# Four graph networks on one core: empty edge places that index spread rows instead of row 0, and attribute scatters dealt out anew

## The chip, the cores and the metric

The kernel runs on one core of one Trainium2 chip, as one program. The metric is the time of one execution on the device in microseconds (us). Engines: PE (matmuls), DVE (VectorE), ACT (ScalarE), POOL (GpSimd, which here issues all indirect DMAs) and SP (SyncE, which issues all plain DMAs).

## The reference

Inputs are 6,250 nodes with 64 features `x`, 100,000 directed edges `src -> dst` (sorted by `dst`) and 18 attributes for each edge. Four networks follow each other; each adds its result to `x`, after a layer norm and a ReLU of its own input.

- Network 0: three layers; a node takes the mean of `h[src]` over its edges by `dst`, then two 64x64 matrices, a batch norm and an ELU.
- Network 1: two attention heads with a scalar score for each edge; sums by `src` of exp(score) times `h[dst]`.
- Network 2: a transformer with 128 hidden features, 8 heads and 4 layers; each layer has an attention over the edges (softmax by `dst`, keys and values gathered by `src`) and then a dense part (gate, layer norm, a 128-512-128 MLP with GELU).
- Network 3: attention with 4 heads, softmax by `src`, keys and values gathered by `dst`; the 18 attributes are projected and added to query, key and value of each edge.

## The kernel before

**Grouping.** Nodes are numbered in 49 blocks of 128 (NP = 6,272 places, 22 of them no node). Edges are padded to EP x ET = 128 x 784 = 100,352; the 352 filler edges have `src = dst = NP - 1`. The kernel sorts edges twice, by block of `dst` (table `tab[0]`, lists `idx[0]`, `node[0]`, `loc[0]`) and by block of `src` (`idx[1]`, ...). Each block's edges fill whole tiles of 128 edges, one edge to a partition, and T = 832 tiles are always processed. Counted from the inputs, 809 tiles hold edges in the order by `dst` (23 at the end are empty) and 810 in that by `src`; the last tile of most blocks is partly empty too, some 3,200 places in all. `idx[k]` holds the row of the node table that the place of an edge gathers. An empty place has local number -1, so that it matches no node, and its `idx` is 0: in order 0 because `fill0`, which `tab[0]` is filled with before edges are scattered into it, is zero in column 0; in order 1 because sums over no edge give 0 (`unpack_dve`, L1025).

**Passes.** A pass over the edges issues 832 indirect gathers from POOL, each 128 rows (one to a partition) into one of 4 buffers: `gathers` (L808) for the three layers of network 0 and for network 1, L1658 in `attend` for the four passes of network 2, L2643 for network 3. The rows are 384, 264, 1,024 and 384 bytes. SP waits for the gathers in the order of the tiles (`landed4` L815, `land_unit` L1676) and then raises a semaphore on which DVE or PE waits. In network 2 the same SP program also issues, behind these waits, the loads of the edge places (L837) and of the flags of the next step (L1666 to L1671), on which DVE's scan L1875 waits. In network 0 PE multiplies a one-hot of each tile by its gathered rows (L1137) and DVE adds (L1113); the third layer begins with `unpack_dve` on DVE. Between two passes lies a dense part, which is a block of its own: a block ends when all engines have ended.

**Attribute scatters.** Network 3 wants the pair and the attributes of each edge in order 1, in `tab[1]`. They are brought there in 49 chunks of 16 indirect scatters from POOL (L728), 784 in all, that are not needed before network 3. `SHARES` deals chunks to places where POOL has nothing else to do: 2 chunks in the dense part of network 0's last layer, 7 behind network 1's pass and in the block `n2i` after it, and 10 with each of network 2's four layers. Of a share of network 2, 32 scatters go behind the pass's gathers, and the rest in the dense block `after(l)`; their rows are loaded by SP (`load_early`: the row numbers and two chunks; `load_late`: the other chunks, two DMAs to a chunk, L701 and L702), and POOL waits for the whole late load before its first scatter in `after(l)`. SP ends `after(l)` with `cols.done`, a wait for all scatters (such waits, whose sums a helper keeps, show as L39).

**Network 1's norm.** The block before network 1's pass has no work for POOL. SP loads weights (L1388, L1389), stores two lists of node numbers (`store`, L1293), reads them back (`load`), and DVE, after the norm, compares them (L1330), builds two score terms with long `tensor_tensor` and `tensor_reduce` operations over 3,136 elements (L1425, L1426), and SP stores the node table (L1398).

Of the kernel before, what the change touches and what calls it, by code (L numbers as in the profile page):

```python
# [6 lines left out]
F32 = mybir.dt.float32  # L7
# [51 lines left out]
def build(nc, d):  # L59
    with ExitStack() as ctx:  # L60
# [40 lines left out]
        def io(pool, out, pat, cm):  # L101
            return pool.iota(out, pat, base=0, channel_multiplier=cm, allow_small_or_imprecise_dtypes=True)
# [45 lines left out]
        def group_edges():  # L148
# [59 lines left out]
            with ExitStack() as st, nc.Block() as block:  # L208
                sig = signals(nc, st, "keys")
                ld, v = sig("ld", 16), sig("v")  # L210

                @block.sync
                def _(sp):
                    for k in range(2):
                        sp.dma_start(ki[:, k, :], keys[k]).then_inc(ld.sem, 16)

                @block.gpsimd
                def _(pool):
                    io(pool, tio, [[1, T]], 0)

                @block.tensor
                def _(pe):
                    pe.matmul(R, zer[:, 0:HR], zer[:, :], start=True, stop=False, skip_group_check=True)

                @block.vector
                def _(dve):
                    v.on(dve.memset(fill, 0))
                    dve.memset(slot_t[:, ET:T], -1.0)
                    dve.memset(slot_p[:, ET:T], -1.0)
                    dve.memset(hi[:, :, ET:ET + 16], 0.0)  # L230
                    dve.memset(lo[:, :, ET:ET + 16], 0.0)
                    v.on(dve.memset(fill0, 0))
                    dve.wait_ge(v.sem, v.c)
                    dve.memset(fill[:, :, 0], -1)
                    dve.memset(fill0[:, :, 1], -1)
                    dve.tensor_scalar(triu, iota[:, :], pcol[:, 0:1], None, ALU.is_gt)
                    dve.wait_ge(ld.sem, ld.up(2))
                    v.on(dve.tensor_scalar(t1, ki, 6, None, ALU.arith_shift_right))
                    v.on(dve.tensor_scalar(ki, ki, LC - 1, None, ALU.bitwise_and))
                    dve.wait_ge(v.sem, v.c)  # L240
                    dve.tensor_copy(hi[:, :, 0:ET], t1)
                    dve.tensor_copy(lo[:, :, 0:ET], ki)
                    ld.back(dve)
                    v.back(dve)

                @block.scalar
                def _(act):
                    act.activation(junk[:, 0, 0:1], pcol[:, 0:1], ACT.Square)
# [484 lines left out]
                if self.n:  # L733
                    sp.wait_ge(sc[0].sem, sc[0].up(16 * self.n))

        SHARES = [0, 0, 2, 7, 10, 10, 10, 10]

        def share(i):
            return Share(sum(SHARES[0:i]), SHARES[i])
# [125 lines left out]
        def network0():  # L865
# [159 lines left out]
            def unpack_dve(dve, s):  # L1025

                def SS(ins):
                    s.on(ins)
                    dve.wait_ge(s.sem, s.c)

                o = STO
                blk, o = area(o, [128, T])
                num, o = area(o, [128, T], I32)
                low, o = area(o, [128, T], I32)
                t = low.bitcast(F32)
                pl = loc[1][:, 0:T]
                SS(dve.tensor_scalar(blk, pl, 128.0, None, ALU.mult))
                for q in range(2):
                    SS(dve.tensor_copy(num[:, 416 * q:416 * q + 416], SORTED[2 + q]))
                SS(dve.tensor_scalar(low, num, 3, None, ALU.bitwise_and))  # L1040
                SS(dve.tensor_copy(node[1][:, :], low))
                SS(dve.tensor_scalar(low, num, 2, None, ALU.arith_shift_right))
                SS(dve.tensor_copy(pl, low))
                SS(dve.tensor_scalar(pl, pl, -1.0, None, ALU.add))
                for q in range(2):
                    r = slice(416 * q, 416 * q + 416)
                    SS(dve.scalar_tensor_tensor(t[:, r], node[1][:, r], 2048.0, SORTED[q], ALU.mult, ALU.add))
                SS(dve.tensor_copy(idx[1][:, 0:T], t))
                SS(dve.scalar_tensor_tensor(blk, pl, 0.0, blk, ALU.is_ge, ALU.mult))
                SS(dve.tensor_tensor(node[1][:, :], blk, pl, ALU.add))  # L1050
                dve.memset(idx[1][:, T:T + 8], 0)
                SS(dve.memset(loc[1][:, T:T + 32], -1.0))
# [294 lines left out]
        def network1(ahead):  # L1347
            o = 0
            TB, o = area(o, [128, B, 66])
            X, o = area(o, [128, 4, 8, 66])  # L1350
            P, o = area(o, [128, 4, 8, 128])
            PT, o = area(o, [128, 2, 8, 128], BF)
            LB0, o = area(o, [128, 1024], BF)
            LB1, o = area(o, [128, 1024], BF)
            LB = [LB0, LB1]
            S3, o = area(o, [128, B, 6], BF)
            tmp, o = area(o, [128, B, 64])
            st_, o = area(o, [128, 4, B])
# [12 lines left out]
            with ExitStack() as st, nc.Block(no_gpsimd_drain=True) as block:  # L1371
                sig = signals(nc, st, "n1")
                v, vard, rootd, ld = sig("v"), sig("vard"), sig("rootd"), sig("ld", 16)
                built, stored = sig("built"), sig("stored", 16)

                f2 = Flags("n2f", sig, 0, 16, rows2, end, 0)
                f3 = Flags("n3f", sig, 1, 16, rows3, f2.o, 4)
                assert f3.o <= WORDS, f3.o

                @block.tensor  # L1380
                def _(pe):
                    f3.turn(pe)
                    f2.turn(pe)

                @block.sync
                def _(sp):
                    for q in range(2):
                        sp.dma_start(wv[:, q, :], bc(d["L1_gnn_W"][q][None, :], [128, 64])).then_inc(ld.sem, 16)  # L1388
                        sp.dma_start(wa[:, q, :, :].rearrange("p a f -> p (a f)"),  # L1389
                                     bc(d["L1_gnn_a"][q][None, :], [128, 128])).then_inc(ld.sem, 16)  # L1390
                    f3.store(sp)
                    f2.store(sp)
                    f3.load(sp)
                    f2.load(sp)
                    f3.finish(sp)
                    f2.finish(sp)
                    sp.wait_ge(built.sem, built.up())
                    sp.dma_start(table.rearrange("(b p) f -> p b f", p=128), TB).then_inc(stored.sem, 16)  # L1398
                    sp.wait_ge(stored.sem, stored.up())
                    built.back(sp)  # L1400
                    stored.back(sp)

                @block.scalar
                def _(act):
                    f3.copy(act)
                    f2.copy(act)
                    norm_act(act, vard, rootd, st_)
                    vard.back(act)

                @block.vector  # L1410
                def _(dve):
                    def VV(ins):
                        v.on(ins)
                        dve.wait_ge(v.sem, v.c)

                    f3.clear(dve)
                    f2.clear(dve)
                    norm_dve(dve, v, vard, rootd, h, x[:, :, :], 64, st_, tmp)
                    f3.compare(dve, v)
                    f2.compare(dve, v)  # L1420
                    dve.wait_ge(ld.sem, ld.up(4))
                    for q in range(2):
                        for s_ in range(2):
                            VV(dve.tensor_tensor(wa[:, q, s_, :], wa[:, q, s_, :], wv[:, q, :], ALU.mult))
                            VV(dve.tensor_tensor(tmp, h, bc(wa[:, q, s_, :][:, None, :], [128, B, 64]), ALU.mult))  # L1425
                            VV(dve.tensor_reduce(S1[:, :, q] if s_ == 0 else TB[:, :, 64 + q], tmp, AX.X, ALU.add))  # L1426
                    dve.sem_inc(built.sem, 1)

                    VV(dve.tensor_copy(S3[:, :, 0:2], S1))
                    VV(dve.tensor_tensor(S1, S1, S3[:, :, 0:2], ALU.subtract))  # L1430
                    VV(dve.tensor_copy(S3[:, :, 2:4], S1))
                    dve.tensor_tensor(S3[:, :, 4:6], S1, S3[:, :, 2:4], ALU.subtract)
                    for s in (v, rootd, ld):
                        s.back(dve)
# [146 lines left out]

            return acc, acc1

        first2 = share(3)
        sums1 = network1(first2)


# [394 lines left out]
        def network2(acc1, acc1b, cols0):  # L1982
# [535 lines left out]

            behind = [Share(sum(SHARES[0:4 + l]), SHARES[4 + l]) for l in range(4)]

            def preload_sp(l, sp, ld):
                sp.dma_start(Wp, d["W2all"][l][:, 512:1536]).then_inc(ld.sem, 16)
# [595 lines left out]
def prepare(inputs):  # L3120
# [2 lines left out]
    a = {}  # L3123

    fill = EP * ET - E
    src, dst = (np.concatenate([f(name), np.full(fill, NP - 1, f(name).dtype)]) for name in ("src", "dst"))
    a["src"], a["dst"] = src.reshape(EP, ET), dst.reshape(EP, ET)
    a["pair"] = np.stack([a["src"], a["dst"]], axis=-1)
    a["attr"] = np.concatenate([f("edge_attr_18"), np.zeros((fill, 18), np.float32)]).reshape(EP, ET, 18)
# [36 lines left out]
```

## Time and profile before

| | us |
|---|---|
| median of 3 runs | 12631.28 (12626.98 to 12631.36) |
| the profiled execution: its own time | 12619.18 |
| the profiled execution: span | 12617.4 |
| POOL busy | 8891.0 (70%) |
| DVE busy | 7916.2 (63%) |
| PE busy | 7549.2 (60%) |
| ACT busy | 6282.0 (50%) |

No engine is busy throughout, and the chain of waits that the page follows back from the end is short, so it does not tell what bounds the kernel. The profile is read stage by stage: which instruction of a stage ends last, and what it waited for. Gathers and scatters from POOL have the operation DMA_INDIRECT. A pause named "issue" is the engine's own time between two instructions.

### The profile page before, as it was taken

How to read it: one execution, taken by the hardware profiler on the slowest of the kernel's cores; microseconds unless marked ns; L12 is line 12 of the kernel's file. 1: busy time of each engine (PE TensorE's matmuls, PEld its weight loads, DVE VectorE, ACT ScalarE, POOL GpSimd, SP SyncE). 2: the span in 40 equal slices, each digit the busy share in tenths (PEclk: the TensorE clock that was granted, in tenths of full speed). 3: DMA queues.
4: the chain of work that ended last, by engine and by line, in shares of the span. 5: the costliest groups of instructions: out<-in, count | busy, mean ns of one | idle time of the engine just before them, and what ended most of it. 6: DMA issues, size and time to landing. Idle time of an engine off the chain costs nothing. (4 is left out here: it accounts for less than half of the span.)

```text
span 12617.4 us, 185971 instructions
## 1 busy us (share of the span) xinstructions
PE 7549.2 (60%) x46394; PEld 5746.9 (46%) x46395; DVE 7916.2 (63%) x21707; ACT 6282.0 (50%) x14083; POOL 8891.0 (70%) x9142
## 2 busy tenths in 40 slices
PE   6666455555551112343666676667666766667998
PEld 5666322232220002333466546663666366645766
DVE  8888666666662224333677767776777677775555
ACT  8333233333333333665566546664666366635666
POOL 0777677767767775777777677776777677766775
PEclk9766677767765555565777787778777877775555
DMA  0000111121121113223444544454444444432223
GB/s 33 2 2 2 31 39 39 39 38 39 39 38 39 40 40 48 54 53 52 132 132 132 118 111 133 131 125 105 132 133 132 96 133 131 133 74 58 72 71 63
DMA packets 820582, 949.30 MB, mean 75 GB/s; under 512 B 481147, under 2 KB 557360, under 8 KB 820156
## 3 DMA queue, kind: packets, MB, share of 16 engines
q0 software_dynamic: 343040, 637.31, 22.0%
q1 hardware_dynamic: 477244, 309.04, 9.2%
q14 instruction: 236, 1.93, 0.0%
q8 instruction: 62, 1.02, 0.0%
HBM read 859.26 MB, written 86.39 MB: 75 GB/s over the span
## 5 line engine op out<-in xcount | busy, mean ns | idle before, releaser
L808 POOL DMA_INDIRECT work<-t,idx x3328 | 3176.7, 955 | 1107.3 <-issue 1014.2
L1658 POOL DMA_INDIRECT work<-t,idx x3328 | 3177.6, 955 | 1024.0 <-issue 1013.4
L820 ACT ACTIVATE work<-iota,loc 128x128 f32<-128x128 f32 (+1 forms) x6672 | 2034.6, 387 | 3253.0 <-DVEq L1110 1921.9
L1113 DVE TENSOR_TENSOR work<-work,ps 128x192 f32 x2496 | 882.8, 354 | 1233.2 <-PE ps L1137 933.6
L1137 PE MATMUL ps<-work 128*128 128x192 bf16 x2496 | 412.7, 305 | 1764.1 <-SPq L815 1702.5
L1753 PE MATMUL ps<-work 128*128 x6784 | 1334.1, 379 | 140.9 <-ACT work L833 81.9
L1753 PEld LDWEIGHTS ps<-work 128*128 128x128 f32 x6784 | 1315.6, 297 | 179.5 <-issue 165.4
L1765 PE MATMUL ps<-work 128*128 128x136 f32 x6656 | 1264.8, 348 | 10.9 <-DVE work L1819 10.1
L600 POOL DMA_INDIRECT tab<-work x784 | 863.1, 1101 | 562.0 <-DVE work L453 315.0
L1137 PEld LDWEIGHTS ps<-work 128*128 128x128 bf16 x2496 | 232.4, 113 | 2077.8 <-issue 1069.8
L728 POOL DMA_INDIRECT tab<-work x784 | 818.7, 1044 | 462.7 <-issue 248.2
L1765 PEld LDWEIGHTS ps<-work 128*128 128x128 f32 x6656 | 1124.2, 246 | 23.2 <-DVE work L1819 15.2
L1849 DVE TENSOR_TENSOR work<-work,ps 128x512 f32<-128x512 f32 x848 | 580.2, 684 | 797.4 <-PE ps L1753 609.5
L2643 POOL DMA_INDIRECT work<-t,idx x832 | 804.7, 967 | 343.7 <-issue 250.2
L1021 PE MATMUL ps<-work 128*128 128x416 f16 x3328 | 995.4, 465 | 83.2 <-DVE work L1012 81.4
L1828 DVE TENSOR_TENSOR work<-work,ps 128x136 f32 x3328 | 939.1, 282 | 75.1 <-DVE work L1828 72.9
L824 ACT ACTIVATE work<-work,ones 128x1024 f32<-128x1024 f32 (+1 forms) x834 | 957.5, 1148 | 27.1
L1519 PE MATMUL ps<-work 128*128 128x130 f32 x1664 | 390.3, 428 | 624.0 <-DVEq L1563 624.0
L1819 DVE TENSOR_TENSOR work<-work,ps 128x512 f32<-128x512 f32 x832 | 567.3, 682 | 135.8 <-DVEq L39 82.5
L1519 PEld LDWEIGHTS ps<-work 128*128 128x128 f32 x1664 | 364.2, 331 | 630.1 <-issue 630.1
L833 ACT ACTIVATE work<-work,ones 128x1024 f32<-128x1024 f32 (+1 forms) x530 | 608.6, 1148 | 65.0 <-ACT work L830 3.4
L1021 PEld LDWEIGHTS ps<-work 128*128 128x128 f16 x3328 | 394.4, 125 | 509.1 <-issue 290.3
(426 smaller groups left out, 17006.6 us busy)
## 6 DMA issues: line engine op xcount, KB each, us to landing
work<-t,idx POOLq DMA_INDIRECT x7488
node<-pl SPq DMA_DIRECT2D x424, 256.0 KB, 3.4
work<-pl SPq DMA_DIRECT2D x54, 512.0 KB
work<-pl SPq DMA_DIRECT2D x106, 256.0 KB, 3.3
tab<-work POOLq DMA_INDIRECT x1568, 2.1
t<-work SPq DMA_DIRECT2D x196, 128.0 KB, 1.8
x<-work SPq DMA_DIRECT2D x196, 64.0 KB, 1.7
h<-work SPq DMA_DIRECT2D x28, 448.0 KB, 2.6
```

The lines of the kernel that those rows point to most:

```text
L600: pool.indirect_dma_start(tab[0], bass.IndirectOffsetOnAxis(ap=rowI[:, u, n:n + 1], axis=0), PAY0[:, u, n, :], None).then_inc(sc[u].sem, 16)
L728: pool.indirect_dma_start(tab[1], bass.IndirectOffsetOnAxis(ap=RI[:, m:m + 1], axis=0), STG[:, 9 - m // 16, m % 16, :], None).then_inc(sc[ ...
L808: pool.indirect_dma_start(X[:, j % 4, n, :], None, table, bass.IndirectOffsetOnAxis(ap=idx[k][:, 8 * j + n:8 * j + n + 1], axis=0)).then_i ...
L820: t = act.activation(P[:, b, n, :], iota[:, :], ACT.Square, scale=-1.0, bias=loc[k][:, bass.ds(a + n, 1)])
L824: act.activation(pv, pv, ACT.Relu, bias=ones[:, 0:1], scale=-1.0).then_inc(made.sem, 1)
L1021: t = pe.matmul(SORTED[2 * i + q], OP[:, 2 * z + m, i, :], OT[:, 2 * z + m, 416 * q:416 * q + 416], start=False, stop=False, skip_group_ch ...
L1113: added.on(dve.tensor_tensor(av, av, part(z, n), ALU.add))
L1658: pool.indirect_dma_start(X[:, j % 4, n, M - KD:W], None, table, bass.IndirectOffsetOnAxis(ap=idx[k][:, NT * j + n:NT * j + n + 1], axis=0 ...
L1753: t = pe.matmul(QK[n // 4][:, n % 4, :], PT[:, z, n, :], q_[:, bass.ds(bp[n], 1), :].rearrange("p a f -> p (a f)"), start=True, stop=True)
L1765: t = pe.matmul(part(n), P[:, 2 * u + n // 8, n % 8, :], X[:, b, n, 0:M], start=True, stop=True)
L1828: v.on(dve.tensor_tensor(av[n % 4], av[n % 4], part(n), ALU.add))
L2643: pool.indirect_dma_start(X[:, j % 4, n, :], None, table, bass.IndirectOffsetOnAxis(ap=idx[k][:, NT * j + n:NT * j + n + 1], axis=0)).then ...
```

## The change

- The 352 filler edges take `src = dst` from the 22 unused numbers 6,250 to 6,271 in turn, instead of all 6,271.
- `fill0`'s column 0, the row that an empty place of order 0 gathers, becomes 4 x partition + tile (an iota on POOL, in the first block after the constants, where a memset on DVE goes).
- `unpack_dve` gets four more DVE operations, which add 4 x partition + tile to `idx[1]` where a place is empty.
- `SHARES` has one more place: 3 chunks in the block of network 1's norm, between the weights' load and the lists' store on SP, and on POOL, which was idle there. The 7 behind network 1's pass stay; network 2's layers get 9, 9, 9 and 10 instead of 10, 10, 10 and 10.
- The `Flags` buffers in that block move to the area of the pass's buffers, which are not in use yet.

```diff
                 def _(pool):
                     io(pool, tio, [[1, T]], 0)
+                    io(pool, fill0[:, :, 0], [[1, TR]], 4)
...
-                    v.on(dve.memset(fill0, 0))
+                    dve.memset(fill0[:, :, 1], -1)
                     dve.wait_ge(v.sem, v.c)
                     dve.memset(fill[:, :, 0], -1)
-                    dve.memset(fill0[:, :, 1], -1)
...
-        SHARES = [0, 0, 2, 7, 10, 10, 10, 10]
+        SHARES = [0, 0, 2, 3, 7, 9, 9, 9, 10]
...
                     SS(dve.scalar_tensor_tensor(t[:, r], node[1][:, r], 2048.0, SORTED[q], ALU.mult, ALU.add))
+                far = num.bitcast(F32)
+                SS(dve.scalar_tensor_tensor(far, pl, 0.0, iotah, ALU.is_lt, ALU.mult))
+                SS(dve.tensor_tensor(t, t, far, ALU.add))
+                SS(dve.tensor_scalar(far, pl, 0.0, pcol[:, 0:1], ALU.is_lt, ALU.mult))
+                SS(dve.scalar_tensor_tensor(t, far, 4.0, t, ALU.mult, ALU.add))
                 SS(dve.tensor_copy(idx[1][:, 0:T], t))
...
             TB, o = area(o, [128, B, 66])
+            passed = o
             X, o = area(o, [128, 4, 8, 66])
...
-                f2 = Flags("n2f", sig, 0, 16, rows2, end, 0)
+                f2 = Flags("n2f", sig, 0, 16, rows2, passed, 0)
                 f3 = Flags("n3f", sig, 1, 16, rows3, f2.o, 4)
-                assert f3.o <= WORDS, f3.o
+                assert f3.o <= kept, f3.o
+                cols = share(3)
+
+                @block.gpsimd
+                def _(pool):
+                    cols.scatter(pool)
...
                         sp.dma_start(wa[:, q, :, :].rearrange("p a f -> p (a f)"),
                                      bc(d["L1_gnn_a"][q][None, :], [128, 128])).then_inc(ld.sem, 16)
+                    cols.load(sp)
                     f3.store(sp)
...
                     sp.wait_ge(stored.sem, stored.up())
+                    cols.done(sp)
...
-        first2 = share(3)
+        first2 = share(4)
...
-            behind = [Share(sum(SHARES[0:4 + l]), SHARES[4 + l]) for l in range(4)]
+            behind = [share(5 + l) for l in range(4)]
...
-    src, dst = (np.concatenate([f(name), np.full(fill, NP - 1, f(name).dtype)]) for name in ("src", "dst"))
+    src, dst = (np.concatenate([f(name), np.resize(np.arange(N, NP), fill).astype(f(name).dtype)]) for name in ("src", "dst"))
```

## Rows read from the trace of the kernel before

**Rows 1.** Groups by line: name, form, count | busy us, mean ns | idle before it, releasers.
```profile
L808 POOL DMA_INDIRECT work<-t,idx x3328 | 3176.7, 955 | 1107.3 <-issue 1014.2 <-POOLq L1371 78.6 <-POOLq L934 7.8
```
**Rows 2.** Timeline, end of network 0's first pass: start us, us, instruction [idle before].
```profile
2559.59 0.94 POOL L808 DMA_INDIRECT work<-t,idx  x1 [0.30 <-issue]
...
2565.48 0.80 PE L1137 MATMUL ps<-work 128*128 128x192 bf16 x4 [2.82 <-SPq L815]
...
2571.93 0.80 PE L1137 MATMUL ps<-work 128*128 128x192 bf16 x4 [2.88 <-SPq L815]
```
**Rows 3.** Windows: stretch, length, busy by engine, PE clock, DMA share, GB/s.
```profile
2400.00:2500.00 100.00, 58.48 (x240) 25.97 (x240) 60.67 (x198) 35.93 (x90) 75.81 (x80) 0.72 0.19 39
2540.00:2560.00 20.00, 9.84 (x36) 4.46 (x34) 9.36 (x30) 0.00 (x0) 15.12 (x17) 0.51 0.91 30
6900.00:7000.00 100.00, 67.36 (x361) 61.91 (x362) 73.56 (x198) 61.52 (x130) 75.94 (x80) 0.74 0.45 132
7160.00:7190.00 30.00, 18.02 (x99) 16.13 (x98) 20.72 (x54) 19.34 (x41) 22.69 (x25) 0.76 0.96 93
```
**Rows 4.** DVE's waits for flags at the four pass ends of network 2 (total, times, longest).
```profile
DVE work L1875 <- DMA work<-sf: 2.5, 2, 2.2
...
DVE work L1875 <- DMA work<-sf: 7.8, 2, 7.5
...
DVE work L1875 <- DMA work<-sf: 5.5, 1, 5.5
...
DVE work L1875 <- DMA work<-sf: 7.1, 1, 7.1
```
**Rows 5.** POOL's waits in network 3's pass (total, times, longest).
```profile
POOL work L2643 <- DVEq L3009: 38.8, 10, 4.1
```
**Rows 6.** SP's waits at the ends of `after(0)`, `after(1)`, `after(2)`.
```profile
SPq L39 <- SPq L39: 14.0, 2, 11.8
...
SPq L39 <- SPq L39: 13.9, 2, 11.2
...
SPq L39 <- SPq L39: 15.2, 2, 12.9
```
**Rows 7.** Windows: scatters alone (L728) in `after(0)` and `n2i`.
```profile
7266.20:7444.10 177.90, 136.37 (x128) 0.96 0.31 91
...
5975.80:6128.00 152.20, 118.37 (x112) 0.80 0.51 115
```
**Rows 8.** SP's waits at the end of `n2i` (total, times, longest).
```profile
SPq L39 <- SPq L39: 5.9, 2, 3.7
```
**Rows 9.** Timeline, first scatter of `after(0)`.
```profile
7266.23 0.96 POOL L728 DMA_INDIRECT tab<-work  x1 [46.23 <-POOLq L39]
```
**Rows 10.** Timeline, network 1's norm and the first instructions behind it.
```profile
4865.18 0.33 SPq L1293 DMA_DIRECT2D n3f_ids<-work  x1
...
4884.07 1.03 DVE L1330 TENSOR_TENSOR work<-work 128x832 f32<-128x832 f32 x1 [3.54 <-DMA work<-n3f_ids]
...
4913.00 3.43 DVE L1425 TENSOR_TENSOR work<-work 128x3136 f32<-128x3136 f32 x1
...
4919.97 0.39 SPq L1398 DMA_DIRECT2D t<-work  x1
...
4936.83 0.98 POOL L808 DMA_INDIRECT work<-t,idx  x1 [78.56 <-POOLq L1371]
4937.03 1.07 SPq L702 DMA_DIRECT2D work<-in_attr  x1
```
**Rows 11.** Timeline, a scatter of `n2i` beside a long DVE operation.
```profile
6001.11 6.79 DVE L2218 TENSOR_TENSOR work<-work 128x6370 f32<-128x6370 f32 x1 [2.80 <-PEq L1436]
6002.31 6.42 POOL L728 DMA_INDIRECT tab<-work  x1 [0.30 <-issue]
```
**Rows 12.** Timeline, `unpack_dve` and the gathers beside it.
```profile
3770.87 1.03 DVE L1049 SCALAR_TENSOR_TENSOR work<-loc,work 128x832 f32<-128x832 f32 x1
...
3771.96 0.94 POOL L808 DMA_INDIRECT work<-t,idx  x1 [0.30 <-issue]
```

More of the change, by code:

```diff
@@ L1355, in network1 @@
             LB = [LB0, LB1]
+            kept = o
             S3, o = area(o, [128, B, 6], BF)
```

## The prediction

> **What bounds the kernel now.** The chain of waits says nothing here, so I read the groups by line first, then the timeline at the end of each pass, then windows and waits there. The groups show that a gather takes 955 ns on POOL and is followed by a pause of its own of 1014.2 / 3328 = 0.305 us, and that almost nothing else stops POOL [rows 1]: one gather in 1.26 us, 832 in 1,048 us. Eight of the nine passes run at that pace. Only network 3's is slower: there POOL waited 38.8 us for a buffer that DVE had not freed [rows 5]. So the middle of a pass can't change; what can are pass ends and the blocks between.
>
> At a pass end the profile shows something odd. In network 0 the DMA engines are busy 0.19 of the time in mid-pass and move 39 GB/s; in the last 20 us before the end they are busy 0.91 and move 30 GB/s. In network 2 it is 0.45 and 132 GB/s against 0.96 and 93 [rows 3]. More occupied and less moved: single reads have become slow. PE, waiting for the landing, takes its last two groups of four tiles 6.45 us apart, which is 1.61 us for a gather instead of 1.26, and multiplies the last one 12.3 us after the last gather was issued [rows 2]. Exactly these gathers are the 23 empty tiles, 128 times row 0, and behind the real edges the 352 filler edges (2.75 tiles), 128 times row 6,271. Nothing else distinguishes them, so I take reads of one row to be what is slow.
>
> Of the dense blocks, `after(0)` to `after(2)` end with SP waiting 11.8, 11.2 and 12.9 us for the scatters alone [rows 6]; `n2i` ends with such a wait too, of 3.7 us [rows 8]. POOL sets their ends.
>
> **Term 1, empty places, network 0: gain 27.** About 25.75 tiles x (1.61 - 1.26) = 9.1 us of backlog stands at each pass end, and PE, DVE and the next dense block follow the landing directly. If spread rows are read like the random rows of mid-pass, the backlog is gone: 3 x 9.1 = 27 us. Bounds: 0 (spread rows as slow) and 30.
>
> **Term 2, the same in network 2: gain 20.** Here DVE and PE run some steps behind the gathers, so the late landing itself is mostly covered. But SP stands in the wait for it, and the next flags are loaded only behind that: DVE's scan waits for them 2.2, 7.5, 5.5 and 7.1 us at the four ends [rows 4], 22.3 together. Some of that is made good by work that piles up meanwhile; I take 20, between 0 and 9.1 x 4 = 36.
>
> **Term 3, the same in networks 1 and 3: 0.** Behind network 1's pass POOL goes straight on with 112 scatters (the count is unchanged), and they end 3.7 us after all else [rows 7, 8]. An earlier landing lengthens only SP's wait. In network 3 DVE is behind the gathers by itself [rows 5]; bounds 0 and 9.
>
> **Term 4, one chunk less in three `after` blocks: gain 36.** The 128 scatters of `after(0)` take 177.9 us, 1.39 each, from 7266.2 [rows 7, 9]. Now there are 9 x 16 - 32 = 112: 155.7 us. The late load is two DMAs shorter, about 1.07 us each on SP [rows 10], so POOL starts about 2 us earlier: near 7264. It then ends near 7420 and lands a little later. The others are ready at 7445.3 - 11.8 = 7433.5, so they become the bound, with 13 us to spare, and the whole wait goes: 11.8 + 11.2 + 12.9 = 35.9 us. The bounds are 3 x 0 (the others turn out to slow down with POOL) and 3 x 24. `after(3)` keeps its 10 chunks.
>
> **Term 5, three chunks in network 1's norm: cost 11.** The block now lasts until the node table is stored, issued at 4919.97 with POOL idle for 78.56 us before the next gather at 4936.83 [rows 10]. Two things come in. SP issues 7 more DMAs (row numbers, 3 x 2) between the weights and the list store at 4865.18; at 0.4 to 1.1 us each this is 3 to 8 us, of which some 3.5 us fall into SP's wait for the lists. The lists come back about 4 us later; DVE already stood idle 3.54 us for them [rows 10], so nothing covers this, and its chain and the table store end 4 us later, at 4940. Second, the 48 scatters start at about 4870, when the first load has landed, and need 48 x 1.26 = 60.5 us if undisturbed: 4930, covered. But they run beside long DVE operations that read two operands from SBUF. The one scatter of the trace that meets such an operation (6.79 us) takes 6.42 us instead of 0.96 [rows 11]: all but 1.3 us of the operation was lost to POOL. Five such operations of 3.43 us follow 4870: 5 x 2.1 = 11 us, with short ones 14. The scatters then end at 4944.5, land at about 4946.5, and the block ends at about 4947 instead of 4936: 11 us. Bounds: 4 (SP's part alone) and 20 (every such operation stops POOL for its full length).
>
> The Trainium skill, GPSIMD Engine Reference, section Specifications, says that GpSimd shares its SBUF interfaces with VectorE and that it contends with instructions in a 2-port perf mode or with two SBUF inputs. The long scatter agrees. By the rule the gathers beside `unpack_dve` should be stopped too, but one issued beside such operations of 1.03 us took its normal 0.94 [rows 12]: short ones cost little. With every listed kind counted in full the norm would cost 18 instead of 11 and the kernel would take 12,567.
>
> **Term 6, small edits: cost 1.** Four DVE operations in `unpack_dve`, about 1 us each [rows 12], lie behind POOL's first 32 gathers (40 us, four free buffers), so no gather waits for them; through the port they may cost 0 to 3 us, I take 1. In the first block an iota on POOL (832 elements elsewhere in that block take under 1 us) replaces a memset on DVE: 0, between a gain of 2 and a cost of 1. The spread empty places inside the passes change neither POOL's pace nor a count: 0. The moved buffers cost nothing.
>
> **The sum.** 27 + 20 + 36 - 11 - 1 = 71 us. On the profiled execution: 12,619 - 71 = 12,548. The median of the runs shown lies 12 us above that execution, so I predict 12,631 - 71 = 12,560 us. A difference under 0.2% (25 us) can't be told from no change here.
>
> **The rivals.**
> - *A, the flags are not what holds network 2's ends.* DVE and PE have a chain of their own in every step; if the wait for flags only replaces one for PE, term 2 is 0: 12,580. For: they are behind anyway. Against: the waits of 5 to 7 us occur once a pass, at the end.
> - *B, spread rows don't help,* because it is the empty rows' place in time and not their address that makes them slow. Terms 1 and 2 go: 36 - 12 = 24 us, 12,607, just inside no change. For: no other gather repeats a row, so the trace can't separate the two. Against: POOL's pace at the end is unchanged.
> - *C, `after` is not shortened,* because PE and DVE get slower or their clock falls when POOL ends earlier: 27 + 20 - 12 = 35, 12,596.
> - *D, slower: spread rows are worse than one row.* In order 0 the 128 places of an empty gather are 4 rows apart, in network 2 a fixed step of 4,096 bytes; if that fell on few memory channels, a gather at a pass end would take longer than 1.61 us. It counts at 7 ends with 25.75 tiles, 180 gathers. The other terms give 24 us, so it decides from 1.61 + 24 / 180 = 1.74 us on; at 2.2 us it costs 106 and the kernel takes 12,713. For: no row shows such a step. Against: mid-pass gathers of 1,024-byte rows use 0.45 of the DMA engines, so they could double in time and still keep up.
> - *E, the norm costs its upper bound or more,* since the table store and the scatters also share the DMA engines: 20 instead of 11, 12,569, inside the forecast's own range; with 16 us more for a store that lasts twice as long, 12,585.
>
> **How the numbers follow.** Forecast with its own range 12,545 to 12,575: 0.68 (here also E's first form). A 0.10, B 0.05, C 0.06, E's second form 0.05, D 0.04, something unnamed 0.02. The range is carried to A and E at 12,590, and down to 12,535 for full gains in terms 2 and 3: it leaves out B, C and D. Faster by over 0.2%: all but B, D and the unnamed, 0.90. Within: 0.06. Slower: 0.04.
>
> **What the changed profile would show.** Term 1: DMA share near 0.2 until the end of network 0's passes, and the last matmuls about 5 us apart and 3 us behind the last gather. Term 2: no wait of the scan for flags over 1 us at network 2's ends. Term 4: SP's wait for scatters in `after(0)` to `after(2)` gone, the last scatter some 13 us before the block's end. Term 5: scatters of 2 to 4 us in network 1's norm and POOL or its landing the last there; between 4 and 20 us more in that block. The prediction fails if the DMA share at pass ends stays above 0.8, or if a block that POOL used to bound ends no earlier.

## The result, and the profile after

The changed kernel takes 12,547.0 us (median of 4 runs, 12,540.65 to 12,556.1), the kernel before 12,631.32 (4 runs, 12,626.98 to 12,636.11): ratio 0.9932, 95% interval [0.9918, 0.9947]. Measured again at the end, beside the last experiment, it took 12,540.86 against 12,615.49: 0.9940 [0.9927, 0.9954]. Forecast were 12,560 us and a gain of 71; the gain is 84 by the medians and 78.5 between the two profiled executions (12,619.18 and 12,540.65). Ten of the twelve experiments ran where every kernel, the one before too, took about 18,070 us, so their totals are set only against the runs of the kernel before made beside them, and they are used mainly for what their traces show.

All terms can be read in the profile after. Line numbers have moved: L1137 is now L1142, L1113 is L1118, L1658 is L1672, L1875 is L1889, L2643 is L2657, L1293 is L1298, L1398 is L1411; the scatter is still L728.

Windows of the changed kernel (columns as in [rows 3]): two stretches in mid-pass and the last 20 us of a pass of networks 0 and 2.
```profile
2400.00:2500.00 100.00, 55.92 (x240) 24.86 (x240) 60.83 (x198) 35.91 (x90) 75.92 (x80) 0.77 0.19 39
2541.00:2561.00 20.00, 11.79 (x48) 5.23 (x48) 11.84 (x38) 0.00 (x0) 15.18 (x16) 0.74 0.19 39
7000.00:7100.00 100.00, 67.20 (x364) 61.77 (x363) 74.22 (x200) 62.11 (x130) 75.93 (x80) 0.76 0.45 132
7144.00:7164.00 20.00, 11.34 (x74) 10.13 (x74) 15.32 (x43) 13.09 (x29) 15.13 (x17) 0.91 0.41 133
```
The end of a pass now looks like its middle: DMA share 0.19 where it was 0.91, and 0.41 where it was 0.96 [rows 3].

The end of network 0's first pass, timeline:
```profile
2557.48 0.49 PE L1142 MATMUL ps<-work 128*128 128x192 bf16 x4 [1.24 <-SPq L815]
...
2559.96 0.94 POOL L808 DMA_INDIRECT work<-t,idx  x1 [0.30 <-issue]
...
2562.51 0.49 PE L1142 MATMUL ps<-work 128*128 128x192 bf16 x4 [2.27 <-SPq L815]
```
PE takes its last two groups 5.03 us apart, not 6.45, and the last of them 2.6 us behind the last gather, not 12.3 [rows 2]. Gather by gather, from the records of the DMA packets: in the kernel before, near the end of a pass of network 0, a gather of real edges lands (its last packet ends) 2.1 to 2.3 us behind its issue. The gathers of filler edges take up to 3.8 us. The first of the 23 empty ones takes 2.9 us again, and each further one some 0.4 us more, up to 11.8 to 12.3 for the last. So the backlog seems to belong to the row: that of row 6,271 does not carry over to row 0. In the changed kernel it is 2.0 to 2.4 us to the end. The next pass starts at 2618.7 instead of 2628.4.

Groups by line, changed kernel: the gathers, network 2's scan, network 3's gathers.
```profile
L808 POOL DMA_INDIRECT work<-t,idx x3328 | 3174.5, 954 | 1034.7 <-issue 1014.4 <-POOLq L934 7.8 <-POOLq L1152 6.4
...
L1889 DVE TENSOR_TENSOR_SCAN work<-tri,ps 128x128 f32<-128x128 bf16 x208 | 86.6, 416 | 4.7 <-DMA work<-sf 2.5 <-PE ps L1786 2.0
...
L2657 POOL DMA_INDIRECT work<-t,idx x832 | 806.3, 969 | 341.0 <-issue 250.5 <-POOLq L2260 55.8 <-DVEq L3023 34.6
```
POOL's pace is the same [rows 1]. The scan's waits for flags, 22.3 us at four ends [rows 4] and 24.9 in the whole kernel before, are 2.5 in the whole changed kernel. Network 3 is held by DVE as before [rows 5].

SP's waits at the ends of `after(0)`, `after(1)` and `after(2)` (total, times, longest):
```profile
SPq L39 <- SPq L39: 2.2, 1, 2.2
...
SPq L39 <- SPq L39: 2.7, 1, 2.7
...
SPq L39 <- SPq L39: 2.2, 1, 2.2
```
The waits of 11.8, 11.2 and 12.9 us for scatters [rows 6] are gone. The 112 scatters of `after(0)` now run from 7242.70 to 7399.20, and the next pass starts at 7411.4. DVE's first operation of that next pass, in the kernel before and then in the changed one, shows what was won:
```profile
7445.91 0.27 DVE L1938 MEMSET x<- 1x256 f32 x1 [25.60 <-PEq L2246]
```
```profile
7410.84 0.27 DVE L1952 MEMSET x<- 1x256 f32 x1 [13.81 <-PEq L2260]
```
DVE stood idle 25.60 us behind its last operation of the block, now 13.81: 11.8 less, which is the whole wait. Counted from the end of the pass's block to the next pass, the three dense blocks are 13.5, 9.6 and 13.6 us shorter, 36.8 together.

Network 1's norm, timeline of the changed kernel:
```profile
4828.20 0.34 SPq L1400 DMA_DIRECT2D work<-in_L_gnn_W  x1
...
4830.95 3.15 SPq L702 DMA_DIRECT2D work<-in_attr  x1
...
4839.44 1.00 SPq L1298 DMA_DIRECT2D n3f_ids<-work  x1
...
4843.64 3.43 DVE L760 TENSOR_TENSOR work<-work 128x3136 f32<-128x3136 f32 x1
4844.35 4.63 POOL L728 DMA_INDIRECT tab<-work  x1 [0.30 <-issue]
...
4864.39 1.03 DVE L1335 TENSOR_TENSOR work<-work 128x832 f32<-128x832 f32 x1 [1.44 <-DMA work<-n2f_ids]
4864.61 1.65 POOL L728 DMA_INDIRECT tab<-work  x1 [0.30 <-issue]
...
4867.46 3.43 DVE L1439 TENSOR_TENSOR work<-work 128x3136 f32<-128x3136 f32 x1
4867.82 3.90 POOL L728 DMA_INDIRECT tab<-work  x1 [0.30 <-issue]
4870.92 3.42 DVE L1440 TENSOR_REDUCE work<-work 128x49 f32<-128x3136 f32 x1
4872.02 0.96 POOL L728 DMA_INDIRECT tab<-work  x1 [0.30 <-issue]
...
4895.97 0.39 SPq L1411 DMA_DIRECT2D t<-work  x1
4919.88 0.35 SPq L707 DMA_DIRECT2D work<-row  x1
```
Counted from the block's first weight load (4828.20; 4859.93 before), the lists are stored at 11.2 us instead of 5.3, the table store is issued at 67.8 instead of 60.0, and the next block starts at 91.7 instead of 76.2 [rows 10]: 15.4 us more. The scatter beside a long operation with two operands lasts until 0.8 us behind that operation's end (1.9 in one case); the one beside the equally long TENSOR_REDUCE, which reads one, takes its 0.96.

SP's waits at the end of this block (total, times, longest), in the kernel before and in the changed one, show two paths that arrive together:
```profile
SPq L39 <- DMA t<-work: 15.4, 1, 15.4
```
```profile
SPq L39 <- DMA tab<-work: 23.1, 1, 23.1
```
By the semaphores, the table store landed 15.8 us behind its issue before and 22.0 in the changed kernel. The last scatter lands only 1.5 us behind the store, 5.7 us behind its own issue. In the second trace of the changed kernel the store takes 20.6 us and the last scatter lands 1.3 us behind it.

Stage by stage, from the starts of the passes in the two profiled executions (gain in us): network 0's passes and dense blocks 10.0, 13.3 and 10.2 (the third up to the first scatter of its dense block), its unpacking -1.1, from that scatter through network 1's norm -15.9, network 1 with `n2i` -0.2, network 2's four stages 18.9, 14.7, 18.9 and 7.8, network 3 2.0, the first block -0.3. The sum is 78.5 before rounding. Network 2's stages split at the end of the pass's block into 5.4, 5.1, 5.3 and 10.2 for the passes (26.0) and 13.5, 9.6, 13.6 and -2.4 for the dense blocks.

### The profile page after: what moved, and what is told of

It reads as the page before. It is cut to its first block and busy times, and to the rows that moved or that the text cites. A ratio compares the mean times of both kernels' runs of the same rounds, so it can differ in the third digit from the quotient of the medians.

```text
span 12538.9 us, 185978 instructions
## 1 busy us (share of the span) xinstructions
PE 7546.9 (60%) x46394; PEld 5740.4 (46%) x46395; DVE 7924.0 (63%) x21710; ACT 6281.8 (50%) x14083; POOL 8905.2 (71%) x9143
## 3 DMA queue, kind: packets, MB, share of 16 engines
q8 instruction: 62, 1.02, 0.0%
## 5 line engine op out<-in xcount | busy, mean ns | idle before, releaser
L1672 POOL DMA_INDIRECT work<-t,idx x3328 | 3180.3, 956 | 1061.6 <-issue 1016.0
L808 POOL DMA_INDIRECT work<-t,idx x3328 | 3174.5, 954 | 1034.7 <-issue 1014.4
L1118 DVE TENSOR_TENSOR work<-work,ps 128x192 f32 x2496 | 883.6, 354 | 1194.5 <-PE ps L1142 896.9
L1142 PE MATMUL ps<-work 128*128 128x192 bf16 x2496 | 411.9, 304 | 1715.6 <-SPq L815 1635.3
L1142 PEld LDWEIGHTS ps<-work 128*128 128x128 bf16 x2496 | 231.3, 113 | 2029.9 <-ACT work L824 1026.9
L728 POOL DMA_INDIRECT tab<-work x784 | 829.5, 1058 | 429.0 <-issue 247.4
L2657 POOL DMA_INDIRECT work<-t,idx x832 | 806.3, 969 | 341.0 <-issue 250.5
```

The costliest lines, as they stand in the source:

```text
L728: pool.indirect_dma_start(tab[1], bass.IndirectOffsetOnAxis(ap=RI[:, m:m + 1], axis=0), STG[:, 9 - m // 16, m % 16, :], None).then_inc(sc[ ...
L808: pool.indirect_dma_start(X[:, j % 4, n, :], None, table, bass.IndirectOffsetOnAxis(ap=idx[k][:, 8 * j + n:8 * j + n + 1], axis=0)).then_i ...
L1118: added.on(dve.tensor_tensor(av, av, part(z, n), ALU.add))
L1672: pool.indirect_dma_start(X[:, j % 4, n, M - KD:W], None, table, bass.IndirectOffsetOnAxis(ap=idx[k][:, NT * j + n:NT * j + n + 1], axis=0 ...
L2657: pool.indirect_dma_start(X[:, j % 4, n, :], None, table, bass.IndirectOffsetOnAxis(ap=idx[k][:, NT * j + n:NT * j + n + 1], axis=0)).then ...
```

## The experiments

### Spread alone, deal alone

```
spread alone: SHARES = [0, 0, 2, 0, 7, 10, 10, 10, 10]    (else the changed kernel)
deal alone:   SHARES = [0, 0, 2, 3, 7, 9, 9, 9, 10], and the old empty places:
-    io(pool, fill0[:, :, 0], [[1, TR]], 4)
+    v.on(dve.memset(fill0, 0))
-    far = num.bitcast(F32)  ... the four operations in unpack_dve
-    np.resize(np.arange(N, NP), fill)
+    np.full(fill, NP - 1)
```


> The change without its new deal of scatters: empty places spread, 10 chunks behind each pass of network 2, none in network 1's norm. Theory 1 (reads of one row queue, and the two halves of the change add up): stage by stage the changed kernel gained 34 us in network 0, 2 in network 3's pass and 60 in network 2, of which 36 are the scatters' waits and 24 the pass ends; so this kernel gains 34 + 24 + 2 - 1 = 59 us, 12,572. Rival (the earlier pass ends of network 2 are worth something only because the blocks behind them no longer wait for POOL): about 35 us, 12,596.

> The new deal of scatters alone, empty places index row 0 as before. Theory 1: 36 us gained in the three dense blocks of network 2, 16 lost in network 1's norm: 20 us gained, 12,611. The backlog of 9 to 12 us at each pass end is back. Rival (the norm's cost comes from the scatters' beginning behind a backlog): a block of network 1's norm nearer to its length before, 30 us gained, 12,601.

> The changed kernel with the old division of the chunks: none in network 1's norm, 10 behind every pass of network 2. What is left of the change is the spread of the empty places. If the pass ends gave what the two traces show stage by stage (33.6 us in network 0, 24.5 in network 2, 2 in network 3, against 1 us more in the unpacking), the gain is 59 us: 12,572 where the kernel before takes 12,631, ratio 0.9953. If the gain of network 2's stages is all that of the shorter scatter blocks, it is 36 us: 12,595.

> The new division of the chunks with the old empty places (rows 0 and 6,271, one row for each). Term 4 less term 5: 36 us less in three blocks, 16 us more in network 1's norm, a gain of 20 us: 12,611, ratio 0.9984. By the forecast's own size of term 5 (11 us) it would be 12,606. If the two parts of the change help each other (the last scatters ended late because the reads of one row were still queued ahead of them), deal and spread alone give less than 84 us together, and this kernel gives under 15 us.

Measured: spread alone 18,034.65 against 18,083.85, ratio 0.9955 [0.9923, 0.9987], and again 18,017.14 against 18,073.55, 0.9973 [0.9945, 1.0002]; deal alone 18,034.31, 0.9983 [0.9953, 1.0013], and again 18,070.29, 1.0002 [0.9980, 1.0025]. By the totals the spread is clear of nothing in the first comparison and at the edge of it in the second, and neither total can tell its 59 us from the rival's 35; the deal alone can't be told from nothing, nor from its 20 us. What decides is the last 20 us of passes. Windows with the spread (mid-pass of network 0, then the end of a pass of network 0 and of network 2):
```profile
3300.00:3380.00 80.00, 35.47 (x156) 17.59 (x156) 39.53 (x127) 24.14 (x63) 47.16 (x50) 0.67 0.15 31
3386.00:3406.00 20.00, 6.89 (x33) 3.35 (x32) 9.81 (x32) 3.59 (x9) 9.97 (x11) 0.73 0.13 28
...
9469.00:9489.00 20.00, 8.52 (x57) 7.97 (x55) 7.52 (x20) 8.00 (x17) 15.24 (x16) 0.75 0.38 120
```
and with the deal alone (the same two pass ends):
```profile
3387.00:3407.00 20.00, 8.71 (x36) 4.16 (x36) 11.59 (x38) 3.59 (x9) 7.60 (x8) 0.66 0.80 30
...
9503.00:9523.00 20.00, 5.46 (x25) 5.27 (x25) 3.58 (x11) 6.29 (x13) 15.22 (x16) 0.63 0.97 93
```
0.80 and 0.97 with one row and the new deal, 0.13 and 0.38 with many rows and the old deal. The other two combinations are the kernel before (one row, old deal: 0.91 and 0.96) and the changed kernel (many rows, new deal: 0.19 and 0.41), so the share follows the rows and not the deal. From the packet records, the last gather of a network 0 pass lands 6.0, 8.8 and 11.8 us behind its issue with one row (10.0, 10.2 and 13.1 in the second run), and 2.0 to 2.2 with the spread. Rival B is false: it is the address.

In the traces of these runs POOL's gathers take as long as ever but stop inside the passes for buffers that DVE has not freed: POOL is idle for 2172.5 us instead of 1034.7 in the passes of networks 0 and 1 of the first run of the spread alone. What a pass end is worth there need not be what it is worth in the result.
```profile
L808 POOL DMA_INDIRECT work<-t,idx x3328 | 3161.7, 950 | 2172.5 <-issue 968.9 <-DVEq L1114 750.7 <-DVEq L1576 328.5
```

### One row for a gather; the same rows for every gather

```
one row for each gather, another for the next:
-    io(pool, fill0[:, :, 0], [[1, TR]], 4)
+    io(pool, fill0[:, :, 0], [[1, TR]], 0)
     and without the term of the partition (pcol) in unpack_dve
the same 128 rows for every gather:
+    io(pool, fill0[:, :, 0], [[0, TR]], 4)
     and without the term of the column (iotah) in unpack_dve
```


> The changed kernel, but the empty places of a gather all index the same row (the tile's number), another one for each gather. Theory 1 (the 128 reads of one gather queue at one row): the DMA share at pass ends is above 0.8 again and the last landing 9 to 12 us behind the last gather; about 55 us of the gain are lost, 12,600. Rival (one row read in gather after gather, thousands of times, is what is slow): as the changed kernel, share 0.2 and 2 us, 12,547.

> The changed kernel, but every empty gather of order 0 reads the same 128 rows (4 p for partition p), so that within one gather no row repeats and between gathers every row repeats. With one row for everything the landing at the pass ends came 6 to 12 us behind the issue, with one row per gather and another for the next it came 3.0 to 3.4 us behind, with all different 2.1 us. If what is slow is many reads of one address at the same time, this kernel shows 2.1 to 2.3 us in all network 0 pass ends and a DMA share under 0.2 there. If it is the return to a row that was read a gather ago, it shows a backlog that grows from gather to gather, to 5 us or more, and a DMA share over 0.5.

The first took 18,010.64 us, the second 18,141.72 (one run each, against 18,083.85 and 18,106.34), which tells nothing: single runs of one kernel differ by as much here. Windows of the first, at a pass end of networks 0 and 2:
```profile
3388.00:3408.00 20.00, 7.42 (x33) 3.67 (x34) 10.56 (x34) 3.59 (x9) 9.34 (x10) 0.72 0.33 27
...
9501.00:9521.00 20.00, 7.70 (x45) 7.35 (x45) 7.94 (x21) 8.10 (x17) 15.12 (x17) 0.67 0.59 118
```
of the second, at the end of network 0's first pass:
```profile
3380.00:3400.00 20.00, 10.00 (x39) 4.74 (x40) 9.91 (x31) 6.65 (x17) 14.92 (x16) 0.67 0.15 37
```
The same 128 rows again and again cost nothing: share 0.15, landing 2.2 us behind the issue. One row in one gather does: share 0.33 instead of 0.13 (0.59 instead of 0.38 in network 2), and the last gather lands 3.2 to 3.4 us behind its issue. But no backlog grows from gather to gather, as it does with one row for all (up to 13.1 us): in network 0 it is 3.2 to 3.6 us from the first of the empty gathers to the last. So what is slow is many reads of one row at the same time, and it becomes a queue when the next gather joins in on that very row. What I had expected of the first kernel, either the whole backlog or none, was too coarse.

### The norm: nothing, loads alone, loads and scatters

```
nothing:      SHARES = [0, 0, 2, 0, 7, 9, 9, 9, 10]   (three chunks are never scattered)
loads alone:  the changed kernel, but POOL only waits for the loads in the norm
-    cols.scatter(pool)
+    pool.wait_ge(early.sem, early.up(5)); early.back(pool)
+    pool.wait_ge(late.sem, late.up(2)); late.back(pool)
-    cols.done(sp)
```


> The changed kernel with no chunks in network 1's norm; three chunks of attributes are never scattered, so part of the work is left out. Theory 1 (the norm's cost is its three chunks and nothing else moved): the next pass starts 16 us earlier, 12,531. Rival (part of it is the lists' new place in memory or the earlier end of network 0): less than 10 us, above 12,537.

> The changed kernel, with the 48 scatters of network 1's norm left out (that part of the table is not written) and SP's seven loads kept. It splits term 5, measured as 15.9 us: if POOL's slowed scatters set the block's end, the next pass starts about 11 us earlier than in the changed kernel and SP's part is some 4 to 5 us; if it is SP's loads and the later lists, the pass starts no earlier and all 16 us remain. In the first case 12,536, in the second 12,547.

The totals, 18,011.56 and 17,952.65 us (one run each), can't carry 6 us; the block itself can, to about 3 us (without chunks it takes 77.1 to 79.8 us here and 76.2 in the profile before). First weight load, table store and next block's first load, without chunks:
```profile
6178.15 0.34 SPq L1400 DMA_DIRECT2D work<-in_L_gnn_W  x1
...
6239.17 0.39 SPq L1411 DMA_DIRECT2D t<-work  x1
...
6257.20 0.35 SPq L707 DMA_DIRECT2D work<-row  x1
```
and with the loads alone:
```profile
6179.98 0.34 SPq L1403 DMA_DIRECT2D work<-in_L_gnn_W  x1
...
6247.40 0.39 SPq L1414 DMA_DIRECT2D t<-work  x1
...
6266.25 0.35 SPq L707 DMA_DIRECT2D work<-row  x1
```
Without chunks 61.0 and 79.0 us, with the loads 67.4 and 86.3. In the four traces of these ten runs with loads and scatters the next block starts 87.8 to 90.7 us after the mark, in the five without chunks 77.1 to 79.8. So the three chunks cost 8 to 13.6 us here, where the two theories of the first experiment had 16 and under 10: not decided. SP's seven loads alone cost 7.2 us (6.5 to 9.2 against the five), nearly twice the 4 of the forecast, and neither expectation of the second experiment is met. The scatters add 1.5 to 4.4 us. If the loads cost as much in the profile after, where the table store goes out 7.8 us later, about 7.7 us are left for the scatters; that is an estimate, and part of it is the slower landing of the store beside them.

### The late wait split

```
SHARES = [0, 0, 2, 0, 7, 10, 10, 10, 10]
-    self.load_chunk(sp, i, late)
+    self.load_chunk(sp, i, third if i == self.few else late)
     if m == 16 * self.few:
-        pool.wait_ge(late.sem, late.up(2 * (self.n - self.few)))
+        pool.wait_ge(third.sem, third.up(2))
+    if m == 16 * self.few + 16:
+        pool.wait_ge(late.sem, late.up(2 * (self.n - self.few - 1)))
```


> Spread rows, the old division of the chunks (none in the norm, 10 behind each pass of network 2), and the wait of the scatters for the late chunks split: for the third chunk alone, and 16 scatters later for the other seven. In the changed kernel POOL is idle at the start of after(0) until 7242.7, when the last of the late chunks has landed, and then needs 156.5 us for 112 scatters; the block ends at 7411.4, 12 us after the last one. With 128 scatters of 1.39 us (178 us) and a start some 15 us earlier, at about 7228, the last ends at about 7406 and lands before the block's other work is done: the three blocks stay as short as in the changed kernel, and the norm gives back its 16 us: 12,531. If the early start only moves the scatters into the time where the 16 loads are still on the DMA engines, or if the start is bound by something else than the late loads, the three blocks end some 10 us later each, and the kernel takes about 12,560.

> The same kernel as in the run of the split wait before (spread rows, none of the chunks in network 1's norm, 10 behind each pass of network 2, the wait for the late chunks split), timed once more, because in the first run the blocks behind network 2's passes were not set by the scatters and the question stayed open. Where the kernel before takes about 12,631, the two theories stand as they did: 12,531 if the earlier start carries the 16 additional scatters at no cost, 12,560 if the three blocks end 10 us later each. Where everything takes about 18,070 again, the total says nothing on it; then only the start of the late scatters is to be read: some 15 to 20 us earlier than with one wait, and the same pace.

18,073.19 against 18,073.55, ratio 0.9986 [0.9959, 1.0013]; again 18,122.70 against 18,106.34, 0.9993 [0.9957, 1.0029]. Inconclusive both times: in these traces the scatters did not set the end of the blocks behind network 2's passes (the last scatter ended 52 to 148 us before the next pass), so the three blocks could not show what was asked. The start did move: in `after(0)` it came 82 us behind the 32 early scatters in the first run, and 100 in both runs with one wait.

### Three chunks loaded a block earlier

```
SHARES = [0, 0, 5, 0, 7, 9, 9, 9, 10]; the late wait split as above
last dense block of network 0:
-    cols.scatter(pool)
+    cols.scatter(pool, 32); carried.append(cols)
-    cols.done(sp)
norm of network 1:
-    cols = share(3)
+    cols = carried[0]
-    cols.load(sp)
```


> The changed kernel, with the three chunks of network 1's norm loaded a block earlier: network 0's last dense block loads five chunks and scatters two of them, and the norm only scatters the other three; the late wait is split as in the run before. SP's seven loads are gone from the norm, so its lists and the table store should be as early as without chunks: 5.3 and 60 to 61 us after the block's first weight load, where the changed kernel has 11.2 and 67.8. The 48 scatters start with the block and not 12 us into it, and now meet the two further long two-operand operations at its head: 60.5 us, 13.7 us of stops as in the changed kernel, 5 us for the new two, and 5 us behind the last one for landing and the block's end: the next block starts 85 us after that mark instead of 90 (87.8 to 91.7 in the runs with 48 scatters, 76.2 to 79.2 without). If POOL's stops are not per long two-operand operation but for the time that the norm runs in all, it stays at 90. Of the whole kernel that is 6 us, less than the comparison can tell.

> The changed kernel itself, beside the kernel before, on the chip of the experiments. Where the kernel before takes 12,631 it should repeat 12,547. Where it takes about 18,070 the parts measured there one by one were a gain of 0.36% for the spread (mean of two runs) and 0.08% for the deal: together 80 us, ratio 0.9956. If the gain depends on POOL being what holds the passes, as it does in the profile before, the ratio is nearer to 1 than 0.9975.

Here the kernel before took 12,615.49 us, as in the result, the changed one 12,540.86 (0.9940 [0.9927, 0.9954]), this one 12,533.39 (12,526.46 to 12,538.6; 0.9934 [0.9920, 0.9947]). It is 7.5 us below the changed kernel, but the runs of the two overlap. Timeline, POOL and SP around the norm, and POOL in `after(0)` (here L731 is the scatter, L1415 the table store):
```profile
4823.48 0.34 SPq L1405 DMA_DIRECT2D work<-in_L_gnn_W  x1
...
4827.37 3.42 DVE L757 TENSOR_TENSOR work<-x,work 128x3136 f32<-128x3136 f32 x1
4827.97 3.65 POOL L731 DMA_INDIRECT tab<-work  x1 [0.30 <-issue]
...
4884.17 0.39 SPq L1415 DMA_DIRECT2D t<-work  x1
4913.36 0.35 SPq L707 DMA_DIRECT2D work<-row  x1
...
7219.79 1.81 POOL L731 DMA_INDIRECT tab<-work  x1 [23.29 <-POOLq L39]
...
7378.89 0.96 POOL L731 DMA_INDIRECT tab<-work  x1 [0.31 <-issue]
7405.81 0.98 POOL L1676 DMA_INDIRECT work<-t,idx  x1 [25.97 <-POOLq L2264]
```
The table store is back at 60.7 us: SP's part is gone. The two long two-operand operations at the head of the norm stop a scatter each, as expected (3.65 and 3.16 us). Yet the next block starts at 89.9, not 85. The gain lies elsewhere: nothing waits at the end of network 0's last dense block any more, it is 9 us shorter (48.0 us from the last gather to the mark, 57.2 in the second trace of the changed kernel), and 54 scatters, not 48, are left for the norm. Both blocks together take 138.5 instead of 147.8 us. POOL sets the end of the pair, through 80 scatters and nine stops: the table store lands 8.8 us before the last scatter, and with the store out of the way that scatter lands 2.1 us behind its issue, not 5.7.

In `after(0)` the scatters start 64 us behind the pass and end 26 us before the next one; in the changed kernel they start 77 us behind it and end 13 us before. The block's length does not follow (250.0 and 246.5 us; the three together 747 and 749). So the block's other work sets its end, as term 4 has it, and 26 us would hold the 16 scatters of a tenth chunk (22 us at 1.39, an estimate). That version, ten chunks behind every pass with none in the norm, has no run in which scatters set the end of these blocks, so this stays untested.

## Why the forecast held, and what it missed

- **Term 1 (27): 33.5.** The cause was right and its size low. The pass ends gave 10.0, 10.3 and 10.2 us: the last gather landed 11.8 to 12.3 us behind its issue and lands 2.1 to 2.2 behind it now, 9.7 to 10.2 us less, where the forecast had 25.75 tiles x (1.61 - 1.26) = 9.1. The 23 empty tiles grow it by 0.4 us each, not 0.35, and the filler tiles add nothing to it. The other 3 us lie in the second pass itself (1,058 and 1,055 us), unexplained.
- **Term 2 (20): about 24.** The four passes' blocks are 26.0 us shorter together; `after(3)`, in which only the spread changed, is 2.4 longer. Rival A, by which the term is 0, is false. But that the flags alone held the ends is argued, not shown: their waits were 2.2, 7.5, 5.5 and 7.1 us and the gains of the passes are 5.4, 5.1, 5.3 and 10.2, alike in the sum and not layer by layer.
- **Term 3 (0): 1.8,** -0.2 and 2.0.
- **Term 4 (36): 36.8,** the waits of 35.9 and 0.9 more. The others did not slow down (rival C), and the last experiment shows that the block's end does not follow when POOL's comes 9 us sooner still.
- **Term 5 (11): 15.9** counted from the first scatter of the dense block before it, 15.4 by the mark: the step whose working was off. By it the next block should start at 87.1 us and starts at 91.7. The scatters need 74.1 us, forecast 74.5, and the stops are 13.7 us, forecast 11 to 14. But they start 2.3 us later, since the loads are slower than 1.1 us each (one took 3.15), and landing and the block's end behind the last scatter take 5.2 us, for which I had 2.5. SP's own part is 7.8 us and not 4 (table store at 67.8, not 60.0), and the store then lands 6.2 us slower than before. It lands 1.5 us before the last scatter, so POOL set the block's end by 1.5 us only. Rival E had named this, the store and the scatters beside each other in the DMA engines; the traces agree with it, but no run separates it.
- **The stops.** I read from [rows 12] that short operations cost little. They do not spare a gather by being short: in the changed kernel's `unpack_dve` three gathers beside operations of 1.02 to 1.03 us took 1.38, 1.25 and 1.39 us. What counts is when the gather begins (last section). The Trainium skill (GPSIMD Engine Reference, section Specifications) names instructions with two SBUF inputs as those that contend with GpSimd. The trace agrees in kind, TENSOR_TENSOR against TENSOR_REDUCE, but the price is at most one stopped scatter for an operation, 2.1 to 3.7 us beside those of 3.43.
- **Term 6 (1): 1.4.**
- **Rival D** (spread rows worse than one) did not come: 0.41 of the DMA engines at network 2's ends.
- **The chances:** B, D and the unnamed are 0.11 together, so "faster" should have been 0.89, not 0.90.

The errors of terms 1 to 4 (+13) and of terms 5 and 6 (-5) partly cancel; what is left is the 7.5 us by which the sum was short. That the total came so near is in part luck.

## What to carry to other kernels

Padding that gathers one and the same row is not free: spread it over rows, and different ones within one transfer (scatters to one row were not tested). Where the DMA engines are busier and move less than a moment before, look at the addresses. Work moved beside another engine's can pay three times: for its loads on the queue (7.2 us here), for the stops beside the other engine's operations (13.7 us), and in the landing of what both send at the same time (the store 22.0 us instead of 15.8, the last scatter 5.7 instead of 2.1).

## What was not expected of the hardware

128 reads of one row in one gather move its landing from 2.2 us behind the issue to between 3.2 and 3.6; the backlog to 12 us comes only when the following gathers want that row too.

A gather or scatter is stopped or not by the moment at which it begins. In the trace of the changed kernel, all 185 that began 0.1 to 0.8 us into a TENSOR_TENSOR of at least 0.9 us with both inputs in SBUF took over 1.1 us instead of 0.95, as a rule until 0.83 us behind that operation's end or the end of the one that followed at once. Of the 30 that began within 0.1 us of its start, on either side, 2 did. Two gathers beside `unpack_dve`, the second behind an operation of the same length:
```profile
3747.23 1.02 DVE L1049 SCALAR_TENSOR_TENSOR work<-loc,work 128x832 f32<-128x832 f32 x1
3747.70 1.38 POOL L808 DMA_INDIRECT work<-t,idx  x1 [0.30 <-issue]
3748.29 1.02 DVE L1050 TENSOR_TENSOR work<-work 128x832 f32<-128x832 f32 x1
...
3749.38 0.94 POOL L808 DMA_INDIRECT work<-t,idx  x1 [0.30 <-issue]
```
The gather of [rows 12], which took its 0.94, began 0.03 us behind the start of an operation that the rows do not show.
